# Four one-hots of a chunk by four one-value comparisons in place of one comparison of two broadcast tiles, in a graph network kernel

## Time and profile before

| | |
|---|---|
| Median of 3 runs | 10777.39 us (10737.08 to 10802.42) |
| The profiled execution | 10759.59 us |
| Its span, first to last instruction | 10757.9 us |
| Mean granted clock of PE | 0.577 |

### The profile page before, as it was taken

The page is one execution under the profiler, slowest core; times in us unless marked ns, Lnnn a source line. Parts: engine busy times, 40 slices in busy tenths (PEclk is TensorE's granted clock), DMA queues, the critical chain, the costliest instruction groups (busy, mean ns, idle before and its releaser), DMA issues. The chain is left out here.

```text
span 10757.9 us, 117227 instructions
## 1 busy us (share of the span) xinstructions
PE 3963.4 (37%) x18072; PEld 3369.1 (31%) x18073; DVE 3958.3 (37%) x9693; ACT 1412.0 (13%) x3057; POOL 5857.7 (54%) x5941
## 2 busy tenths in 40 slices
PE   1343423334330155533344443333323333233332
PEld 1333322333330155500233333333323333233332
DVE  5335554444441166697112111212132222422224
ACT  1000011111110144475100000000000000000000
POOL 0666775555557500077566666666635555356653
PEclk6555556666665565655665565555555555555555
DMA  1111112333330133300212111111111111111111
GB/s 43 44 42 42 44 30 70 92 92 97 92 89 19 27 91 90 86 1 8 65 52 56 53 56 43 44 44 44 42 39 41 41 41 40 35 41 42 43 41 38
DMA packets 364723, 548.61 MB, mean 51 GB/s; under 512 B 124102, under 2 KB 217114, under 8 KB 364650
## 3 DMA queue, kind: packets, MB, share of 16 engines
q0 software_dynamic: 186368, 330.08, 12.3%
q1 hardware_dynamic: 148330, 190.56, 5.9%
q10 hardware_dynamic: 29952, 27.28, 1.0%
HBM read 448.36 MB, written 99.13 MB: 51 GB/s over the span
## 5 line engine op out<-in xcount | busy, mean ns | idle before, releaser
L685 PE MATMUL PS<-GATHERED,OH 128*128 128x128 f32 (+1 forms) x10240 | 2424.9, 418 | 4047.4 <-issue 1531.1
L685 PEld LDWEIGHTS PS<-GATHERED,OH 128*128 128x128 f32 x10240 | 2154.0, 313 | 4369.5 <-issue 1797.3
L571 POOL DMA_INDIRECT GATHERED<-row_tab,IDX x2496 | 2459.1, 985 | 1934.5 <-issue 1039.2
L571 POOL DMA_INDIRECT GATHERED<-gat_tab,IDX x832 | 784.8, 943 | 750.9 <-DVEq L1567 462.5
L571 POOL DMA_INDIRECT GATHERED<-typed_tab,IDX x832 | 830.5, 998 | 500.6 <-issue 243.2
L591 POOL DMA_INDIRECT list_dram<-REC_NOW,PLACE_NOW x832 | 925.7, 1113 | 310.1 <-issue 263.0
L571 POOL DMA_INDIRECT GATHERED<-typed_b_tab,IDX x832 | 806.7, 970 | 448.4 <-issue 259.3
L1244 DVE TENSOR_SCALAR OH<-IOTA,DSTF,WF 128x128 f32 x2048 | 602.3, 360 | 979.4 <-issue 947.5
L751 PE MATMUL PS<-IDENT,GATHERED 128*128 128x128 f32 x3328 | 588.7, 355 | 932.4 <-DVEq L1567 749.4
L751 PEld LDWEIGHTS PS<-IDENT,GATHERED 128*128 128x128 f32 x3328 | 542.9, 188 | 978.2 <-issue 975.1
L1260 DVE TENSOR_TENSOR X<-X,PS 128x128 f32 x512 | 146.4, 286 | 1661.9 <-remote 1119.9
(11 more groups left out here) (251 smaller groups left out, 4102.1 us busy)
## 6 DMA issues: line engine op xcount, KB each, us to landing
gat_rows<-GATHERED SPq DMA_DIRECT2D x208, 264.0 KB
GATHERED<-gat_rows SPq DMA_DIRECT2D x208, 264.0 KB
GATHERED<-row_tab,IDX POOLq DMA_INDIRECT x2496
ROWI<-dst_rows ACTq DMA_DIRECT2D x208, 128.0 KB
ROWI<-dst_rows SPq DMA_DIRECT2D x208, 128.0 KB
list_dram<-REC_NOW,PLACE_NOW POOLq DMA_INDIRECT x832
GATHERED<-gat_tab,IDX POOLq DMA_INDIRECT x832
GATHERED<-typed_tab,IDX POOLq DMA_INDIRECT x832
```

Source lines behind the costliest of these rows:

```text
L571: pool.indirect_dma_start(out=rows, out_offset=None, in_=table, in_offset=bass.IndirectOffsetOnAxis(ap=IDX[:, k:k + 1], axis=0),).then_inc ...
L685: last = mm(bank(to + p)[:, 0:r.shape[1]], onehots_(p, t), r, start=(t == 0), stop=(t == CT - 1))
```

## The change

In l0, l2 and l2b a chunk's one-hots are made by four comparisons of 128 columns, each with one value per partition (the target's column), where one comparison of 512 columns stood. gb keeps the wide form, l3a and l3b keep theirs. Lines after the first added one are shifted: L1238 to 1244 become L1239 to 1250, and the add of L1260 is L1265.

```diff
--- before.py
+++ after.py
@@ -88,6 +88,7 @@
     BIG = 1e30
     FAR = 2.0 ** 50
     LIF_T = 25
+    UNWEIGHED = "unweighed"
     SLOTS = 4
     REGS = 4
     assert NB % SLOTS == 1
@@ -1241,8 +1242,12 @@
                                            column[:, bass.ds(c * CT, CT)].rearrange("p (t o) -> p t o", o=1)
                                            .to_broadcast([P, CT, P]), ALU.is_equal)
                 for t in range(CT):
-                    last = v.tensor_scalar(onehot(p, t), IOTA[:, bass.ds(b * P, P)], DSTF[:, bass.ds(c * CT + t, 1)],
-                                           weights[:, bass.ds(c * CT + t, 1)], ALU.is_equal, ALU.mult)
+                    if weights is UNWEIGHED:
+                        last = v.tensor_scalar(onehot(p, t), IOTA[:, bass.ds(b * P, P)], column[:, bass.ds(c * CT + t, 1)],
+                                               None, ALU.is_equal)
+                    else:
+                        last = v.tensor_scalar(onehot(p, t), IOTA[:, bass.ds(b * P, P)], column[:, bass.ds(c * CT + t, 1)],
+                                               weights[:, bass.ds(c * CT + t, 1)], ALU.is_equal, ALU.mult)
                 return last
 
             def all_added(wk, banks, table):
@@ -1483,7 +1488,7 @@
                 chunk_table(RANGEF_SRC, RANGES_SRC)
 
             dve.sem_inc(counted, 1)
-            aggregate("l0", lambda b: ACC[:, bass.ds(b * XW, D + 1)], D + 1,
+            aggregate("l0", lambda b: ACC[:, bass.ds(b * XW, D + 1)], D + 1, UNWEIGHED,
                       parts=((NIT // 2, count, bucket_starts), (NIT // 2 - 1, rank, places)))
 
             ts(small(12), A3[:, :, D], 1.0, None, ALU.add)
@@ -1723,10 +1728,10 @@
             for s in (nb_turned, nb_ht, nb_mm, nb_made):
                 dve.sem_inc(s, 1)
             dve.sem_inc(nb_stored, 16)
-            aggregate("l2", lambda b: X[:, bass.ds(b * D, D)], D, column=DST2[:, :])
+            aggregate("l2", lambda b: X[:, bass.ds(b * D, D)], D, UNWEIGHED, column=DST2[:, :])
             dve.sem_inc(walks["l2b"].free, RING)
             dve.wait_ge(list_in, 16)
-            aggregate("l2b", lambda b: X[:, bass.ds(b * D, D)], D, column=LIST_SRC, table=RANGES_SRC)
+            aggregate("l2b", lambda b: X[:, bass.ds(b * D, D)], D, UNWEIGHED, column=LIST_SRC, table=RANGES_SRC)
 
 
             norm_relu()
```

## The result

| | kernel before | changed kernel |
|---|---|---|
| median, us | 10786.2 (4 runs, 10737.1 to 10802.4) | 11219.3 (4 runs, 11177.6 to 11238.9) |
| profiled span, us | 10757.9 | 11175.9 |
| ratio | | 1.0408, 95% interval 1.0377 to 1.0439 |

The account below looks back on a forecast made before the run. No engine was full; POOL's gathers, their stretch and POOL's pauses were taken to bound the gather walks. Terms 82 + 70 + 41 - 20 = +173 us on 10759.6 made 10933, given as 10930, range 10690 to 11110.

Parts of the forecast that it names:

- The change, part by part: The prediction's pricing of the change: DVE's datapath, DVE's queue, then terms for l2b, l2 and both halves of l0.
- l2b, +82 forecast: Walk l2b: longer by the mean of l3a's +97 us and l3b's +67 us over it, +82 us.
- the 0.42 us a one-hot of the term: DVE in each walk: 0.69 us becomes 1.11 us a one-hot, 108 us more work a walk, mostly hidden.
- The signs named: In l2b, if right: gathers of 946 ns, POOL's pauses for DVE 230 to 290 us, comparisons 1.4 us apart in bursts.
- l2, +70: Walk l2: the same price as l2b, less 12 us more regained from its more stretched gathers, +70 us.
- l0, +41 and -20: Walk l0: first half, half of 82, +41 us; second half, POOL bound and the wide comparisons' stretch gone, -20 us.
- The sign named for the wrong case: l0's ranking half longer by more than 40 us, meaning that DVE's queue and not POOL bounds it.
- The narrow form as a whole, +173: Sum of the terms for l2b, l2 and l0's two halves, +173 us.
- Rival 1: Gather walks: only the stretch goes and pauses stay as in l2b, -77 us, so 10683; chance 0.15.
- Rival 3: All 130 laps of l2, l2b and l0's first half pause 8.05 us: 542 less 77, so 11225; chance 0.05.
- Rival 4: Narrow comparisons hold up gathers by 0.34 us, one per one-hot: 261 us on POOL, 11194; chance 0.03.
- The rule of the Trainium skill that was weighed there: GpSimd and VectorE share one port pair, locked by a two-port-mode VectorE instruction, or two SBUF inputs against GpSimd's SBUF read.

Follow-up runs that it names:

- the run with l0 wide: The changed kernel with l0's one-hots wide again, so narrow only in l2 and l2b: 10865.2 us, 1.0036 of the kernel before.
- shifts of 102, 128 and 230: The kernel before with 102, 128 or 230 idle semaphore increments on DVE's queue ahead of gb: 11170.9 us (1.0313), 10847.0 us (1.0023), 11161.7 us.
- the run with increments alone: The kernel before, one-hots wide, with five idle increments ahead of each one-hot of l0, l2 and l2b, and 8 ahead of gb: 10938.9 us, 1.0096.
- breaks of increments on POOL's queue: The kernel before with 16 idle increments behind every second chunk's gathers, or 2 behind every gather, on POOL's queue: 10773.3 us (0.9948) and 10776.1 us (0.9952).
- the shift of 92: The kernel before with 92 idle semaphore increments on DVE's queue ahead of gb: 9024.2 us, some 272 us more, at the lower level.

## Why the prediction was wrong, point by point

**The step that failed is the first sentence of "The change, part by part": "Only DVE's one-hots in l0, l2 and l2b change."** True of the diff's instructions, not of their places. gb had no term, and none of the rivals had one; it took 319 us of the 418. The count of DVE's instructions was in front of me, and so was the queue that brings them; I read neither against the loops that follow l0.

**l2b, +82 forecast.** +50 in the profiled pair. DVE's datapath took less than the 0.42 us a one-hot of the term: its busy time grew by 207 us over 768 one-hots, 0.27 each. The signs named came: gathers of 946 ns, POOL's wait for DVE 245 us (230 to 290 was given), comparisons 1.4 us apart in bursts. The walk took 1297 us, under the 1310 to 1345 named.

**l2, +70.** +11 in the profiled pair; for both walks 39 us by the run with l0 wide, against 152. The price was read from l3a and l3b minus l2b, one sample of each walk. From first to last freed slot those two walks were 1341 and 1311 us in the profile before; in the eight other profiles at the upper level that leave their code and POOL's alone, l3a came out at 1285 to 1315 and l3b at 1297 to 1330. In the three of these with l2b as it was (shifts of 102, 128 and 230) l3a is 21, 27 and 42 us longer than l2b and l3b 36, 36 and 58, some 37 us in place of my 82. More than half of the price was the chance of one execution. (From first to last gather l2b takes 1247 to 1279 us in the four profiles of this level where it is wide and nothing is added to it or to POOL's queue, and 1279 to 1297 in the five where it is narrow.) The mechanism behind it, that DVE's count of instructions makes the bursts cost more, was right, and the run with increments alone shows it (+0.96%).

**l0, +41 and -20.** First half +20 (from 644 to 665 us, first gather to the 427th), which is inside what this half varies by without a change: 644 to 676 us in the profiles with l0 as it was. Second half +17 (from 611 to 628), where a gain was forecast, and this holds in the other profiles of this level (from the 427th gather to the last 609 to 615 us with l0 wide and nothing added to it, 621 to 631 with it narrow): beside the ranking too the bursts took back what the stretch gave. The sign named for the wrong case, 40 us or more longer, did not come.

**The narrow form as a whole, +173.** Between 61 us (1.0057) and 132 us (1.0123) at this level; the difference of the changed kernel's ratio and that of the shift by 102, 0.0095, is 102 us, across two sessions. Too high in each case, right in sign.

**Rival 1** (only the stretch goes, -77 us) is what happens at the lower level: -68 us in the median, of which 13 are the neuron loop's, and l0, l2 and l2b shorter by 22, 19 and 26 us from first to last freed slot. **Rival 3** gave 11225 and the result is 11219, by accident: laps did get longer, but by 6.8 us in gb and not by 4.17 in the typed walks. **Rival 4** is excluded: 946 ns beside narrow comparisons, and none of l2b's gathers longer than 1047 ns. The rule of the Trainium skill that was weighed there (SBUF — State Buffer, section SBUF: two separate sides) is borne out for the wide form (984 and 969 ns become 945 and 946). Its other half, the two-port mode, is not, if the narrow comparison with its one source runs in that mode; which mode it runs in no run here shows.

**What stays open:** what sets the level, and why at the upper one the queues are slow while POOL issues indirect DMAs, why breaks of increments on POOL's queue gain half a per cent there, and why two sessions put the narrow form at 0.6 and at 1.2%.

## What to carry to other kernels

An edit that adds or removes instructions moves every loop behind it on that engine. For each loop of more than two pieces of 128 instructions, read the packets of the instruction queue in its stretch, before and after: a loop that fetches in every lap has a cost which no dependence shows, and some idle increments ahead of it are the cheap test (26 of them gave 3.5% back). Do that before judging the edit: here it hid a form that is 0.8% faster in one condition of the chip. And price a form by walks of one execution only if you have seen how much the same walk varies between executions.

## What the runs showed of the hardware

- DVE's instructions come in packets of 8192 bytes, by the two loops and their shifts 128 instructions each. A DVE loop of 270 instructions (294 in the listing, with its jumps) is loaded once if it lies within three pieces of 128, and fetches five packets a lap if it reaches into a fourth; that costs 5.5 us a lap with the shift of 92 and 6.8 with that of 102 (laps of 23.5 and 24.7 us against 17.9 to 18.1). Nearly all of it stands in one gap of a lap.
- A narrow comparison (one tile, one pointer, 128 x 128) does not stretch a gather beside it: means of 945 to 951 ns in l2 and l2b, the first three of l2 left out; the wide one of two tiles does, 964 to 1010.
- The same program took 10,828 and 8,750 us on one chip in two sessions. The upper level has steps of the queues of up to 1.4 us (DVE's register steps of one line, median 0.18 in both) and POOL pauses of over 2 us once a lap; the lower has neither. In gb, at the upper level, the slow steps end with POOL's last indirect DMA: 69 of 103 register steps of DVE over 0.5 us before it and none of 1568 after it, in the kernel before. An edit's sign can differ between the two, so the level belongs beside every ratio.
